# Attention in a fused two-layer kernel: half of the statistics and of the normalisation moved to later in each step, an opening in another order, SyncE's sequence reordered

## What is computed

```python
x = x + L0_xattn(layernorm(x), ctx, ctx, ...)  # 16 heads of 32, softmax over 128 keys, output projection
x = x + L0_ffn(layernorm(x), ...)              # quantised, 512 -> 2048 -> 512
x = x + L1_xattn(layernorm(x), ctx, ctx, ...)  # attention without softmax, layer norm
x = x + L1_ffn(layernorm(x), ...)              # three 512 x 512 matmuls, tanh
```

## Time and profile before

| | |
|---|---|
| median of 3 runs | 1847.01 us (1843.23 to 1847.41) |
| profiled execution, its own time | 1845.27 us |
| its span, first to last instruction | 1843.4 us |
| TensorE busy | 1752.3 us (95%) |
| VectorE busy | 1559.2 us (85%) |
| ScalarE busy | 1226.8 us (67%) |
| GpSimd busy | 969.8 us (53%) |
| attention, first scores to last `out` | from 172 to about 933 us |

### The profile page before, as it was taken

The page is one execution under the profiler, slowest core; times in us unless marked ns, Lnnn a source line. Parts: engine busy times, 40 slices in busy tenths (PEclk is TensorE's granted clock), DMA queues, the critical chain, the costliest instruction groups (busy, mean ns, idle before and its releaser), DMA issues. The chain is left out here.

```text
span 1843.4 us, 29839 instructions
## 1 busy us (share of the span) xinstructions
PE 1752.3 (95%) x9082; PEld 1305.8 (71%) x9162; DVE 1559.2 (85%) x3587; ACT 1226.8 (67%) x3374; POOL 969.8 (53%) x1076
## 2 busy tenths in 40 slices
PE   8897799999999999999879999889999999999997
PEld 7775678888888888888644444357777777777775
DVE  6865689999999999988769888888888988888885
ACT  4574799999999999999733333265655655665543
POOL 2333356666666666666610000047776776677664
PEclk9998899999999999999989999999999999999999
DMA  8665345565556555644379999154455455454311
GB/s 302 195 217 159 97 108 140 154 155 141 140 156 157 137 140 150 155 116 117 90 228 390 397 400 392 72 209 158 159 173 179 156 173 182 153 173 162 129 58 40
DMA packets 154478, 323.13 MB, mean 175 GB/s; under 512 B 47440, under 2 KB 55632, under 8 KB 136656
## 3 DMA queue, kind: packets, MB, share of 16 engines
q1 hardware_dynamic: 154176, 320.96, 54.9%
q10 hardware_dynamic: 144, 0.26, 0.0%
HBM read 164.90 MB, written 105.91 MB: 147 GB/s over the span
## 5 line engine op out<-in xcount | busy, mean ns | idle before, releaser
L1287 POOL TENSOR_TENSOR a_pr<-a_pr,a_rcp 128x512 f32<-128x512 f32 x256 | 266.4, 1041 | 239.7 <-DVE a_rcp L1132 239.5
L1037 ACT ACTIVATE a_pr<-a_s,a_nmax 128x128 f32<-128x128 f32 x1024 | 364.9, 383 | 25.7 <-DVE a_nmax L1125 23.6
L1037 ACT ACTIVATION_READ_ACCUMULATOR a_pr<-a_s,a_nmax 128x1 f32 x1024 | 227.6, 222 | 0.0
L1538 PE MATMUL f_pair<-f_room,w 128*128 128x512 bf16 x999 | 223.9, 381 | 2.6 <-ACT f_room L1649 1.3
L1957 POOL TENSOR_TENSOR f_rs<-f_rs,f_half 128x1 f32<-128x1 f32 x128 | 121.2, 947 | 179.2 <-DVE f_rs L1804 179.2
L1758 DVE CUSTOM_DVE_ANT_0 f_hf<-f_pair,nb,sh 128x512 f32<-128x512 f32 x244 | 172.4, 747 | 27.5 <-PE f_pair L1538 27.2
L1687 ACT ACTIVATE f_room<-f_ring,f_off,f_rs 128x511 f32<-128x511 f32 (+1 forms) x128 | 104.4, 816 | 119.8 <-POOL f_off L1963 119.8
L1140 DVE TENSOR_TENSOR a_pTl<-a_pt,a_pTh 128x512 fp32r<-128x512 f32 x256 | 168.4, 679 | 17.1 <-ACT a_pTh L1049 17.0
L937 PE MATMUL a_pt<-ident,a_pr 128*128 128x128 f32 x1024 | 160.2, 279 | 22.4 <-POOL a_pr L1287 15.0
L1125 DVE TENSOR_REDUCE a_nmax<-a_s 128x4 f32<-128x512 f32 x256 | 171.7, 671 | 11.5 <-PE a_s L925 11.1
L1538 PEld LDWEIGHTS f_pair<-f_room,w 128*128 128x128 bf16 x1024 | 99.2, 98 | 115.9 <-issue 2.1
(11 more groups left out here) (389 smaller groups left out, 5005.0 us busy)
## 6 DMA issues: line engine op xcount, KB each, us to landing
hidden<-f_hf SPq DMA_DIRECT2D x57, 1024.0 KB, 8.1
f_hf<-hidden SPq DMA_DIRECT2D x57, 1024.0 KB, 4.8
xb<-x SPq DMA_DIRECT2D x16, 1024.0 KB, 5.8
ctxh<-bqreph SPq DMA_DIRECT2D x128, 128.0 KB, 2.3
a_xr<-x SPq DMA_DIRECT2D x64, 256.0 KB, 3.7
x<-a_xr SPq DMA_DIRECT2D x64, 256.0 KB, 2.4
f_ring<-x SPq DMA_DIRECT2D x64, 256.0 KB, 3.3
out<-f_ring SPq DMA_DIRECT2D x64, 256.0 KB, 2.6
```

Of the source, the lines that this page charges most:

```text
L1037: last = e.activation(pr[:, t, j, :], s_bank[t][:, j * P:j * P + P], ACT.Exp, bias=nmax[kk % 2][:, t, j:j + 1], accum_out=sums[kk % 2][:, ...
L1287: e.tensor_tensor(p, p, rcp[kk % 2][:, t, :].unsqueeze(2).to_broadcast([P, 4, KEYS]), ALU.mult).then_inc(*e_pn)
L1538: last = e.matmul(h_bank[(PAIRS * u + i) % 3][:, q, :], w1[:, k, f * P:f * P + P], xT[u % 2][:, k, :], start=k == 0, stop=k == KC - 1)
```

## The change

In every step VectorE's `stats` and `norm` are split in halves: one statistics instruction (A: tile 0, B: tile 2) or two normalisations stay where all were, and the others (A: tile 1; B: tile 3, and the four aggregates that end the group; N: tiles 2 and 3) go between `xlo` and `plo(2)`. `rc(2)` goes ahead of `xlo`. GpSimd's `clo` of a step goes into the next step, behind `prob(1)`, with two buffers `cs` in place of one; `rstd` goes from step B to behind `rstd1` of step N. SyncE's step has the order `again`, `vals`, `paired`, `keys`, `store`, `load`.

In the opening (step 0 of batch 0) the transposes of chunks 4 and 5 write the two banks of `v_bank`, idle then, and the queries follow them without waiting for `xlo`; all statistics of group 2 come before step 0. At the end of `prepare`, five of the eight transfers of the first queries are issued by ScalarE, and three by SyncE behind the barrier. `sw2row`, a row of scales that only `rest` reads, goes through memory instead of staying in SBUF.

```diff
+            def send_queries():
+
+                e_half_hi.wait_ge(e, 28)
+                e_clear.wait_ge(e, 0)
+                for plane, to, at, n in QUERY_BLOCKS[0]:
+                    e.dma_start(f32(query_planes(scr, 0)[plane][to:to + n, :]), f32(q0[0])[at:at + n, :])\
+                        .then_inc(scr["e_qs"][0].sem, 16)
 
...
-            for h in range(2):
-                if h == 0:
-                    e_half_hi.wait_ge(e, 28)
-                else:
-                    e_gone.wait_ge(e, by_dve[place["q"][0]])
-                for plane, to, at, n in QUERY_BLOCKS[h]:
-                    e.dma_start(f32(query_planes(scr, 0)[plane][to:to + n, :]), f32(q0[h])[at:at + n, :])\
-                        .then_inc(scr["e_qs"][0].sem, 16)
+            e_gone.wait_ge(e, by_dve[place["row"][0]])
+            e.dma_start(scr["sw2row"], sw2row[:]).then_inc(*scr["e_sw2"])
...
+        AHEAD = {TURNED: v_bank[0], TURNED + 1: v_bank[1]}
...
-                if first(b) and o == TURNED:
-                    e_qlo.wait_ge(e, 1 - ASKED)
-                elif there(b, kk + QUERY) and not (first(b) and kk < 0):
+                if first(b) and o in AHEAD:
+                    pass
+                elif there(b, kk + QUERY):
                     e_qlo.wait_ge(e, b * TPB + kk + QUERY - ASKED)
                 else:
                     e_xlo.wait_ge(e, b * TPB + o - 1 - TURNED)
-                bank = x_bank
...
-                    if not first(b) or o > ASKED:
+                    if first(b) and o == ASKED + 1:
+                        e_qlo.wait_ge(e, 0)
+                    elif not first(b) or o > ASKED:
...
                     xt(b, -1)
-                else:
-                    queries(b, kk, 1)
+                    queries(b, kk, 0)
+                queries(b, kk, 1)
                 scores(b, kk, 2)
-                if opening:
-                    queries(b, kk, 0)
-                    queries(b, kk, 1)
...
                     xhi(b, -1)
-                else:
-                    qhi(b, kk)
+                qhi(b, kk)
                 vlow(b, kk)
                 exp(b, kk, 2)
-                if opening:
-                    qhi(b, kk)
-                else:
+                if not opening:
                     xhi(b, kk)
                 phi(b, kk, 2)
...
-                e_clo.wait_ge(e, u - 1)
+                e_clo.wait_ge(e, u - 2)
                 e_vl.wait_ge(e, 2 * u + i)
                 at = slice(64 * i, 64 * i + 64)
-                e.tensor_tensor(cs[at, :], v_bank[i][at, :], vl[at, :], ALU.add).then_inc(*e_vs)
+                e.tensor_tensor(cs[o % 2][at, :], v_bank[i][at, :], vl[at, :], ALU.add).then_inc(*e_vs)
...
-            def stats(b, kk, ahead, tiles, group):
+            def stats(b, kk, ahead, t):
...
-                e_x[g % 2].wait_ge(e, half_of(b, g) - (1 - g % 2))
-                for t in tiles:
-                    last = e.bn_stats(st[:, t, :], xb[g % 2][:, t, :])
-                last.then_inc(*e_bn)
-                e_bn.wait_ge(e, 2 * (G - NORMED) + group)
+                if t == 0:
+                    e_x[g % 2].wait_ge(e, half_of(b, g) - (1 - g % 2))
+                    e_mv.wait_ge(e, G - NORMED - 1)
+                e.bn_stats(st[:, t, :], xb[g % 2][:, t, :]).then_inc(*e_bn)
+                if t < TPG - 1:
+                    return
+                e_bn.wait_ge(e, TPG * (G - NORMED) + t)
                 e.memset(tick[:], 0.0)
-                for t in tiles:
-                    last = e.bn_aggr(mv[g % 2][:, t, :], st[:, t, :])
+                for i in range(TPG):
+                    last = e.bn_aggr(mv[g % 2][:, i, :], st[:, i, :])
                 last.then_inc(*e_mv)
 
-            def norm(b, kk):
+            def norm(b, kk, tiles):
                 o = kk + NORM
...
-                for t in range(TPG):
+                for t in tiles:
                     last = e.tensor_scalar(xb[g % 2][:, t, :], xb[g % 2][:, t, :], mv[g % 2][:, t, 0:1],
                                            rs[g % 2][:, t:t + 1], ALU.subtract, ALU.mult)
-                last.then_inc(*e_xn)
+                if t == TPG - 1:
+                    last.then_inc(*e_xn)
 
...
+                    if kk == -1:
+                        for t in range(TPG):
+                            stats(b, kk + t // 2, (LN_A, LN_B)[t // 2], t)
...
-                    stats(b, kk, LN_A, (0, 1), 0)
-                    stats(b, kk, LN_B, (2, 3), 1)
-                    norm(b, kk)
+                    stats(b, kk, LN_A, 0)
+                    stats(b, kk, LN_B, 2)
+                    norm(b, kk, (0, 1))
                 rc(b, kk, 1)
                 smax(b, kk, 2)
                 qlo(b, kk)
                 vsum(b, kk, 0)
                 smax(b, kk, 3)
                 vsum(b, kk, 1)
+                rc(b, kk, 2)
                 if not opening:
                     xlo(b, kk)
-                rc(b, kk, 2)
+                    stats(b, kk, LN_A, 1)
+                    stats(b, kk, LN_B, 3)
+                    norm(b, kk, (2, 3))
                 plo(b, kk, 2)
                 plo(b, kk, 3)
                 if opening:
                     xlo(b, kk)
-                    stats(b, -1, LN_A, (0, 1), 0)
-                    stats(b, kk, LN_B, (2, 3), 1)
                 x1_stats(b, kk)
             body_steps(e, step, LOAD, STORE)
             keep(NB - 1, HALF)
...
                 prob(b, kk - 1, 3)
                 rstd1(b, kk)
+                rstd(b, kk - 1)
                 prob(b, kk, 0)
                 prob(b, kk, 1)
+                clo(b, kk - 1)
                 xbo(b, kk)
-                rstd(b, kk)
                 prob(b, kk, 2)
-                clo(b, kk)
             body_steps(e, step, LOAD, STORE + 1)
...
                 o = kk + QUERY
-                if not there(b, o) or first(b) and o < ASKED:
-                    return
-
-                e_s.wait_ge(e, 4 * (b * TPB + o - 2) + 3)
+                if not there(b, o):
+                    return
+
+                if not first(b) or kk >= 0:
+                    e_s.wait_ge(e, 4 * (b * TPB + kk) + 3)
                 for h, e_half in ((0, e_qhi), (1, e_qlo)):
-                    e_half.wait_ge(e, b * TPB + o - ASKED)
+                    if first(b) and o < ASKED and h == 0:
+                        continue
+                    if not first(b) or o >= ASKED:
...
             def step(b, kk):
+                again(b, kk)
+                if first(b) and kk == 0:
+                    e_const.wait_ge(e, 0)
+                    vals(b, kk - 1)
+                if not first(b) or kk >= 0:
+                    vals(b, kk)
                 paired(b, kk)
+                keys(b, kk)
+                store(b, kk)
                 load(b, kk)
-                store(b, kk)
-                again(b, kk)
-                if first(b) and kk == VALUE - 2:
-                    e_const.wait_ge(e, 0)
-                vals(b, kk)
-                keys(b, kk)
 
             body_steps(e, step, LOAD, STORE + 1)
             for t in range(4):
...
+            e.dma_start(sw2row[:], scr["sw2row"]).then_inc(*e_sw2)
```

More of the change, by code:

```diff
@@ L119, in prepare @@
         ones = sb("ones", [P, P])
+        sw2row = sb("sw2row", [P, D])
         st, mv = sb("st", [P, 2, TPG, 6]), sb("mv", [P, 2, TPG, 2])
@@ L403, in _ @@
             e.activation(q0[0], bank[p % 6][:], ACT.Identity, bias=scr["bq"][:, 0:1]).then_inc(*e_half_hi)
+            send_queries()
         @block.vector
@@ L580, in _ @@
             e_prod.wait_ge(e, p)
-            e.tensor_copy(scr["sw2row"][:], bank[p % 6][:]).then_inc(*e_gone)
+            e.tensor_copy(sw2row[:], bank[p % 6][:]).then_inc(*e_gone)
             norm(1)
@@ L773, in _ @@
             e_keys.wait_ge(e, KEYS_HERE * len(KEY_BLOCKS) - 1)
+            scr["e_sw2"].wait_ge(e, 0)
 def body_steps(e, fn, before, after, per=TPB):
@@ L816, in attend @@
         vp = [vp_room[:, 4 * P * c:4 * P * (c + 1)].rearrange("p (j n) -> p j n", j=4) for c in range(KC)]
-        cs, vl = sb("cs", [P, 512]), sb("vl", [P, 512])
+        cs, vl = [sb(f"cs{i}", [P, 512]) for i in range(2)], sb("vl", [P, 512])
         xb = scr["xb"]
@@ L874, in out_bank, with turn_bank @@
             return idle_bank[w % 4] if last_group(w) else o_bank
+        def turn_bank(b, o):
+            return AHEAD.get(o, x_bank) if first(b) else x_bank
         def half_of(b, g):
@@ L909, in xt @@
                     e_xlo.wait_ge(e, b * TPB + o - 1 - TURNED)
-                bank = x_bank
+                bank = turn_bank(b, o)
                 for t in range(TPG):
@@ L1029, in xhi @@
                 e_xt.wait_ge(e, b * TPB + o - TURNED)
-                e.activation(xT[o // 4 % 2][0][:, o % 4, :], x_bank[:], ACT.Copy).then_inc(*e_xhi)
+                e.activation(xT[o // 4 % 2][0][:, o % 4, :], turn_bank(b, o)[:], ACT.Copy).then_inc(*e_xhi)
             def exp(b, kk, t):
@@ L1078, in chi @@
                 e_vs.wait_ge(e, 2 * u + 1)
```

(18 more changed lines are left out.)

3 lines of the change are left out of this document (2 added, 1 removed).

## The result

| | median, us | runs | profiled execution: span |
|---|---|---|---|
| before | 1845.63 | 1843.23 to 1847.41, 4 | 1843.4 |
| after | 1860.2 | 1859.91 to 1860.82, 4 | 1859.0 |

The ratio is 1.008, 95% interval 1.0063 to 1.0098: slower by 14.6 us. 1859.5 was predicted, as 13.1 us more than before.

The account below looks back on a forecast made before the run. The prediction took a closed ring through VectorE, ScalarE and TensorE as the bound. Steady steps +24.5, opening −12.4 and tail +1.0 gave +13.1 us: 1858.4 or 1860.1 by base, taken as 1859.5, range 1841 to 1872.

Parts of the forecast that it names:

- The ring: Steady attention steps: closed chain through VectorE, ScalarE and TensorE, slack at most 0.1 us; work behind xlo lengthens the step.
- A: Steady step with statistics of tiles 0 and 1: one bn_stats of 0.60 moved into the ring, step longer by 0.51 us.
- B: Steady step with statistics of tiles 2 and 3: one bn_stats, memset and four aggregates moved, step longer by 0.99 us.
- N: Steady step that normalises: two norm instructions moved cost 0.87 us, less its present lateness of 0.33.
- a pair takes about 0.96: Normalising step: length in us of the two moved norm instructions, taken from four lasting 2.01.
- POOL's order, 0: Steady steps: later clo and rstd delay neither out nor a probability, so they cost 0 us.
- Group 3, 0 (−0.3 to +2): Steps 3 to 5, before x1_stats runs: VectorE's branch is shorter by about what is inserted, so 0 us.
- rival 3: Steady steps: new waits lower TensorE's clock in every third of 36 longer steps, +17 us, 1876; chance 0.06.
- SyncE's order, 0 (−1.5 to +4): Attention steps: later loads could delay POOL's probability, or late steps could cease; taken as 0 us.
- The tail, +1.0: Last four tiles: out waits for the last clo, now behind rstd1 of the next step; +1.0 us (0.3 to 1.5).
- The opening, −12.4: Start to values(1): earlier entry, idle banks, early statistics and later rstd save 12.4 us (bounds −7 and −14).
- The rest: FFN part: sw2row through memory adds one hidden 256 KB load, 0 us (bounds 0 and 0.6).

Follow-up runs that it names:

- 1: Changed kernel with all statistics and all four norm instructions back in the first half, ahead of rc(1); 1840.7 us, ratio 0.9973 to the kernel before.
- 3: Changed kernel with all statistics, aggregates and four norm instructions in the second half, behind xlo; 1886.54 us, ratio 1.0218 to the kernel before.
- experiment 7: Changed kernel with rc(2) put behind the second half's statistics and norm; 1860.6 us, ratio 1.0077 to the kernel before.
- 6: Changed kernel with POOL's order (rstd, clo) as in the kernel before, VectorE's halves kept; 1878.45 us, ratio 1.017 to the kernel before.
- 11: Changed kernel with clo back behind prob(2) of its own step, rstd left as changed; 1857.33 us, ratio 1.0062 to the kernel before.
- 5: Changed kernel with all statistics and norm in the first half and POOL's order as before; 1833.76 us, ratio 0.994 to the kernel before.
- experiment 2: Kernel before with only the halved statistics and norm and rc(2) ahead of xlo, POOL's order as before; 1890.14 us, ratio 1.0238.
- 8: Changed kernel with steady statistics and norm in the first half and POOL's old order, rstd a step late for group 2 alone; 1835.5 us, ratio 0.9944.
- experiment 12: The joint version 8 with rc(2) behind xlo again in the steady steps; 1833.93 us, ratio 0.9932 to the kernel before.
- experiment 4: Changed kernel with the first steps' banks, order and early group 2 statistics undone; query transfers and rstd's place kept; 1866.71 us.

## Why the prediction was right, step by step

- **The ring** was right, and the runs show it: undone (1), doubled (3). A: +0.51 predicted, +0.52 measured. B: +0.99 and +0.92. By the medians of the four kinds of step the twelve groups cost 26.7 us, not 24.5; that the stretch shows 25.3 is luck, for three steps of the kernel before were late by 1.5 us together in the one trace (below).
- **N** was +0.54 and is +0.79. The term that was mis-sized is "a pair takes about 0.96": beside POOL's probability the second half's pair takes 1.29, and 0.99 without it (7). With `norm` split and POOL's old order N is 12.02 (6), 0.45 over the kernel before where I had 0.54; nearly all of the other 0.34 is that meeting, 0.30 by experiment 7. Of it 0.14 comes from the late `clo` (11), which I had costed at 0 in the steady steps: it doesn't delay `out`, as I had walked, but it delays the probability that `norm` then meets.
- **POOL's order, 0**, was right only as a sum inside the changed kernel. Alone it costs: with whole norm +0.55 in N (1 against 5). And without it the halves cost 1.2 us more in B (2, 6). I had costed each of the two edits as if the other stood still.
- **Group 3, 0 (−0.3 to +2)**, was wrong: step 4 costs +1.9, near the upper bound. I had reasoned that VectorE's branch is shorter there by what is inserted. The runs show in its place a TensorE wait that grows from 1.73 to 2.22 and a clock that falls behind it, in each of the nine kernels with work in the second half and in none of the five without. This is rival 3's mechanism, which I had priced for the steady steps alone.
- **SyncE's order, 0 (−1.5 to +4)**: the three late steps of the kernel before (10, 46, 50: 11.68, 12.03, 11.50) have none to answer to them in the changed kernel, 1.5 us. But experiment 2 keeps the old order and has 11.24 in all three, and experiments 5, 8 and 12 have the new order and a late step 33 (12 also a late 17). So nothing ties these steps to SyncE's order; no kernel here changes that order alone.
- **The tail, +1.0**: +0.96, and −0.92 when undone (11), at the same clock.
- **The opening, −12.4**: −13.2. The first query matmul is 2.1 earlier (1.9 predicted; the eleven experiments with the new entry have it at 164.2 to 166.1, the one with the old at 166.76; that scatter is almost as large as the gain, so its size is not shown), the first scores 1.5. 6.9 is banks, order and statistics. The other 4.8 (28.93 less 24.18) lie between the kernel before and experiment 4: `rstd` ahead of the probability, which holds two probabilities until 193.87 and, behind their `pt`, six query matmuls that experiment 4 runs before its last wait, and a granted clock of 0.50 from 195 to 198, after the idle time there, against 1.00 from 188 on in experiment 4 (which had its own 0.50 earlier, from 174.5 to 182.5). That last split is argued from the two traces and not tried. My walk had these as parts of one line and couldn't tell them apart.
- **The rest**: the FFN part took 896.7 us from its first hidden matmul in the trace before and 899.0 in the one after. The twelve kernels of the experiments took 896.9 to 898.8, and experiment 2, which has none of the store and load of `sw2row`, 897.8, in the middle. Five kernels with them took 896.9 to 897.6. So the 2.3 us are not `sw2row`'s. They go with the clock: it rises 2.87 us after that first matmul in the kernel before and 5.84 after it in the changed one, and the other twelve kernels lie between, the later the rise the longer the part. Why it rises later in one trace than in another stays open.
- **Rival 3, the clock**, came true in one early step (+1.9) and in no steady one; experiments 2 and 6 have it in four steady B each, where TensorE waits 2.00 us in one piece.
- **The number** is closer than its terms. The predicted difference was 13.1 and the measured one 14.6 (15.6 in the spans). 1859.5 is 0.7 from 1860.2 because I had set it between two bases, 1845.27 and 1847.01, while the four times of the kernel before have a median of 1845.63: on that the sum gives 1858.7. And step 4 and the part behind attention (+1.8 each), both predicted at 0, are partly made up by the late steps and step 62 of the kernel before.

## What to carry to other kernels

Before work is moved on an engine with spare time, find which of its gaps lies behind the last link of the closed chain: the same 0.60 us instruction cost nothing ahead of `xlo` and 0.58 behind it. Then ask of each moved result which other engine stands in line for it: the halves alone cost 45 us, where with the consumer moved as well the steady steps cost 27. And split a mixed change into its halves on the chip: the opening here was worth 13 us, the steady part cost 25, and experiment 12 keeps the one without the other. Last, look at the early steps by themselves: where TensorE idles already, a wait that is half a microsecond longer cost a clock step and 1.9 us.
